# Attention operands through memory, maxima three units ahead, scaled sums early: one change to a tuned attention and gated feed-forward kernel

## The reference, cut to what matters

```
x : 4 x 512 x 512, float32
x = layernorm(x + attention(x))    # 32 query heads of 16, 8 key/value heads: 4 query heads share one
x = layernorm(x + ffn(x))          # 1792 inner rows in blocks of 32; a rank-16 product picks one row per block

attention: q, k, v = x @ wq, x @ wk, x @ wv
           out = softmax(q k^T / 4) v ;  out @ wo
ffn:       inter = x @ c1^T @ c2^T ;  idx = argmax in each block of 32
           h = relu(w1[idx] . x)   ;  out = sum_k h[k] * w2[idx[k]]
```

## Time and profile before

| | us |
|---|---|
| median of three runs | 1025.3 |
| the profiled execution | 1030.88 |
| its span | 1029.1 |
| TensorE's granted clock, mean | 0.895 of 2.4 GHz |

### The profile page before, as it was taken

How to read it: one execution, slowest core, us unless ns; L and a number is a source line. 1 busy time by engine, 2 the same in 40 slices (tenths; PEclk the granted TensorE clock), 3 DMA queues, 4 the chain that set the end, 5 groups by cost and what they waited for, 6 DMA issues and landing times. The chain is left out here.

```text
span 1029.1 us, 12101 instructions
## 1 busy us (share of the span) xinstructions
PE 894.3 (87%) x4344; PEld 528.1 (51%) x4344; DVE 573.5 (56%) x782; ACT 428.3 (42%) x789; POOL 296.7 (29%) x370
## 2 busy tenths in 40 slices
PE   7989888997689889898886546899999999999995
PEld 5755333332233233232324335677777777777774
DVE  6466758876477767776711555643274346426313
ACT  4314655775476656665760101133322222222221
POOL 1002436222333212654630322233421122222221
PEclk9989976988798878878986668999999999999998
DMA  4420522333523333434315245222112003001101
GB/s 143 105 70 3 125 52 59 74 68 70 140 54 67 68 72 58 115 77 97 83 32 153 97 146 172 80 64 82 41 48 75 1 1 103 1 1 42 42 0 41
DMA packets 49243, 72.61 MB, mean 71 GB/s; under 512 B 13888, under 2 KB 18496, under 8 KB 48672
## 3 DMA queue, kind: packets, MB, share of 16 engines
q1 hardware_dynamic: 41552, 65.57, 24.1%
q0 software_dynamic: 7632, 6.28, 2.7%
HBM read 35.31 MB, written 17.56 MB: 51 GB/s over the span
## 5 line engine op out<-in xcount | busy, mean ns | idle before, releaser
L476 DVE TENSOR_REDUCE neg_max<-ps_max 128x2 f32<-128x1024 f32 x256 | 305.9, 1220 | 106.5 <-PE ps_max L589 105.9
L444 ACT ACTIVATE probs<-ps_st 128x512 f32<-128x512 f32 x512 | 270.5, 600 | 147.5 <-PE ps_st L602 145.6
L602 PE MATMUL ps_st<-q,k 50*128 50x512 f32 x512 | 172.8, 539 | 40.6 <-DMA q<-maxima 36.9
L602 PEld LDWEIGHTS ps_st<-q,k 50*128 50x128 f32 x512 | 80.1, 214 | 210.8 <-ACT probs L444 145.1
L616 PE MATMUL ps_pv<-probs,v 128*32 128x512 f32 x1024 | 164.0, 718 | 2.4 <-ACT probs L444 2.4
L291 POOL DMA_DIRECT2D maxima<-max_rows x128 | 77.8, 615 | 265.6 <-DVE max_rows L498 264.9
L846 POOL TENSOR_TENSOR g_l<-picked,g_h 128x512 fp32r<-128x512 f32 x56 | 73.0, 1304 | 269.2 <-ACT g_h L898 269.2
L589 PE MATMUL ps_max<-k,q 48*128 48x512 f32 x512 | 121.2, 488 | 26.1 <-DVE neg_max L476 21.7
L884 ACT ACTIVATE mask_t<-ps_t 128x512 bf16<-128x512 bf16 x56 | 33.4, 597 | 172.7 <-PE ps_t L1113 172.7
L947 DVE TENSOR_REDUCE top<-ps_prep 128x14 f32<-128x448 f32 x62 | 38.6, 623 | 99.7 <-PE ps_prep L1088 99.6
L589 PEld LDWEIGHTS ps_max<-k,q 48*128 48x128 f32 x512 | 62.3, 219 | 58.5 <-DVE neg_max L476 40.2
(11 more groups left out here) (139 smaller groups left out, 1163.2 us busy)
## 6 DMA issues: line engine op xcount, KB each, us to landing
q<-parts SPq DMA_DIRECT2D x192, 64.0 KB, 2.4
sums<-stage SPq DMA_DIRECT2D x32, 256.0 KB, 2.5
k<-parts SPq DMA_DIRECT2D x192, 32.0 KB, 2.0
x_raw<-xT SPq DMA_DIRECT2D x16, 256.0 KB, 4.7
yf<-x SPq DMA_DIRECT2D x4, 1024.0 KB, 5.6
after_attention<-yf SPq DMA_DIRECT2D x4, 1024.0 KB, 10.1
yf<-after_attention SPq DMA_DIRECT2D x4, 1024.0 KB, 5.4
w_raw<-w POOLq DMA_DIRECT2D x16, 224.0 KB, 3.1
```

The costliest lines, as they stand in the source:

```text
L444: nc.scalar.activation(probs[kt % 2][:, r], ps_st[i % 3][:], ACT.Exp, scale=float(HD) ** -0.5).then_inc(exp_done, 1)
L476: nc.vector.tensor_reduce(neg_max[:, at:at + 2], ps_max[pair % 2][:], AX.X, ALU.max, negate=True).then_inc(max_red, 1)
L602: nc.tensor.matmul(ps_st[i % 3][:], k_[n % QR][64 * a:64 * a + ROWS, kt * P:(kt + 1) * P], q[n % QR][64 * a:64 * a + ROWS, j, :], start=Tr ...
```

## The change

1. Operands: after the projections of a batch, SP stores `parts` (high and low of keys and queries, 10 KB rows) to a DRAM buffer `operands`, two DMAs per batch (`store_parts`). A unit is loaded from there by eight DMAs instead of twelve: four on SP (partitions 0 to 47) and four on Pool (partitions 64 to 111). `parts` has two buffers instead of four, so tasks of batch 2 and 3 wait for the stores of batch 0 and 1.
2. `AHEAD = 3`: first passes run three units ahead, with five operand tiles (`QR = 5`). The projections carry 24 pairs instead of 16. The maxima of units 0 and 1 are turned within the projections, and those of unit n + 2 in unit n.
3. The maxima go to DRAM by one DMA instead of four.
4. Denominators are loaded in unit 8b + 9, inverted in 8b + 11, stored and reloaded in 8b + 12 and 8b + 13, for b = 0, 1, 2; Pool scales in unit 8b + 14 and makes both parts in 8b + 15. Only batch 3 is left for the second block, where Pool makes its low part.
5. The w1 splits run one per unit in units 5 to 20.
6. The second block's order changes: denominators are loaded first, both output projections of batch 0 and 1 come first on PE, and Pool's order is root(0), scale, low parts, root(1).

```diff
-    QR = 4
+    QR = 5
+    AHEAD = 3
-    RING = 3 * TILES
-    LOADS = 12
+    RING = (AHEAD + 1) * TILES
+    LOADS = 4
...
+            def store_parts(b):
+                sp.wait_ge(low_out, (REP + 1) * (b + 1))
+                dst = operands[b * PARTS:(b + 1) * PARTS].rearrange("(g h d o t) -> h g d (o t)", g=NKV, h=2, d=HD, t=S)
+                for h in range(2):
+                    sp.dma_start(dst[h], parts[b % 2][:, :, h].bitcast(F32)).then_inc(part_out[b % 2], DMA)
...
             def load_unit(n):
                 if g == 0:
-                    sp.wait_ge(low_out, (REP + 1) * (b + 1))
-                src = parts[b][HD * g:HD * (g + 1)].bitcast(F32)
-                for a in range(2):
-                    for c in range(3):
-                        rows = slice(64 * a + HD * c, 64 * a + HD * (c + 1))
-                        sp.dma_start(k_[j][rows].bitcast(F32), src[:, 0, (0, 0, 1)[c]]).then_inc(unit_in[j], DMA)
-                        sp.dma_start(q[j][rows].bitcast(F32), src[:, 1 + a::2, (0, 1, 0)[c]]).then_inc(unit_in[j], DMA)
+                    sp.wait_ge(part_out[b % 2], 2 * DMA * (b // 2 + 1))
+                at = b * PARTS + g * PARTS // NKV
+                rows = operands[at:at + PARTS // NKV].rearrange("(r o t) -> r o t", r=2 * HD, t=S)
+                for a in (0,):
+                    k_at, q_at = k_[j][64 * a:64 * a + STACK].bitcast(F32), q[j][64 * a:64 * a + STACK].bitcast(F32)
+                    sp.dma_start(k_at[0:2 * HD], rows[0:HD, 0].rearrange("d (c t) -> c d t", c=1).broadcast_to(
+                        [2, HD, S])).then_inc(unit_in[j], DMA)
+                    sp.dma_start(q_at[0:2 * HD], rows[:, 1 + a::2]).then_inc(unit_in[j], DMA)
+                    sp.dma_start(k_at[2 * HD:STACK], rows[HD:2 * HD, 0]).then_inc(unit_in[j], DMA)
+                    sp.dma_start(q_at[2 * HD:STACK], rows[0:HD, 1 + a::2]).then_inc(unit_in[j], DMA)
...
             for k in range(KT):
                 load_x(1, k)
+            store_parts(0)
+            for k in range(KT):
+                load_x(2, k)
             load_unit(0)
             for k in range(KT):
-                load_x(2, k)
+                load_x(3, k)
+            store_parts(1)
             load_unit(1)
             load_unit(2)
-            for k in range(KT):
-                load_x(3, k)
+            store_parts(2)
+            load_unit(3)
+            store_parts(3)
             for n in range(NU):
-                if n + 3 < NU:
-                    load_unit(n + 3)
+                if n + AHEAD + 1 < NU:
+                    load_unit(n + AHEAD + 1)
                 if n:
                     store_unit(n - 1)
-                if n in DEN_AT:
-                    load_den(DEN_AT[n])
-                if n - 1 in DEN_AT:
-                    store_reciprocals(DEN_AT[n - 1])
-                if n == 11:
-                    load_att()
+                b, at = divmod(n - NKV, NKV)
+                if b >= 0 and at == 1:
+                    load_den(b)
+                if b >= 0 and at == 4:
+                    store_reciprocals(b)
+                if b >= 0 and at == 5:
+                    load_att(b)
...
             def send_shift(n):
-                for o in range(4):
-                    pool.dma_start(dst[o], max_rows[32 * o:32 * (o + 1)]).then_inc(max_out, DMA)
-                pool.wait_ge(max_out, 4 * DMA * (n + 1))
+                pool.dma_start(to.rearrange("(c o x) -> o c x", c=32, o=4), max_rows[:]).then_inc(max_out, DMA)
+                pool.wait_ge(max_out, DMA * (n + 1))
...
+            for n in range(AHEAD + 1):
+                load_unit(n)
             send_shift(0)
+            send_shift(1)
             for n in range(NU):
-                if n + 1 < NU:
-                    send_shift(n + 1)
+                if n + AHEAD + 1 < NU:
+                    load_unit(n + AHEAD + 1)
+                if n + 2 < NU:
+                    send_shift(n + 2)
...
-                if n == 12:
-                    scale()
-                if n == 14:
-                    low_att()
-                for i in range(KT * NC):
-                    if 22 + i // 2 == n:
-                        split_w1(i)
+                if 5 <= n < 5 + KT * NC:
+                    split_w1(n - 5)
+                b, at = divmod(n - NKV, NKV)
+                if b >= 0 and at == 6:
+                    scale(b)
+                if b >= 0 and at == 7:
+                    split_att(b)
...
-            for t in range(TT):
-                project_out(0, t)
-            project_out(1, 0)
-            project_out(1, 1)
+            for b in range(2):
+                for t in range(TT):
+                    project_out(b, t)
+            project_out(2, 0)
             front(0)
             front(1)
-            project_out(1, 2)
+            project_out(2, 1)
             front(2)
             front(3)
-            project_out(1, 3)
+            project_out(2, 2)
             front(U)
...
```

More of the change, by code:

```diff
@@ L52 @@
 NU = NB * NKV
+WQ = D + 2 * KV
+PARTS = 2 * P * (REP + 1) * S
 def _scratch(nc, name, n):
@@ L114, in _attend @@
         with ExitStack() as early:
-            x3 = [early.enter_context(nc.sbuf_tensor(f"x_{part}3", [P, KT, S], F32R)) for part in "hl"]
+            first_f = early.enter_context(nc.sbuf_tensor("first_f", [P, P], F32))
         stage = [sb(f"stage{j}", [P, S]) for j in range(2)]
+        with ExitStack() as late:
+            att, inv = [late.enter_context(nc.sbuf_tensor(name, [P, REP, S], F32)) for name in ("att", "inv")]
         wo_raw, c2_raw = sb("wo_raw", [P, REP, D]), sb("c2_raw", [80, INTER])
         c1_raw = sb("c1_raw", [P, KT, 80])
-        w1_raw = [sb(f"w1_raw{j}", [P, CH]) for j in range(2)]
         ps_max = [ps(f"ps_max{j}", [P, 2, S]) for j in range(2)]
@@ L339, in split_w1 @@
                 if i == 0:
-                    pool.wait_ge(att_split, REP)
-                    for j in range(QR):
-                        pool.wait_ge(unit_in[j], LOADS * DMA * (NU - NKV) // QR)
                     load_w1(0)
@@ L402, in take_task @@
                     return
-                nc.scalar.activation(parts[b][:, o, 0], bank(i)[:], ACT.Copy).then_inc(high_out, 1)
+                if b >= 2 and o == 0:
+                    act.wait_ge(part_out[b % 2], 2 * DMA * (b // 2))
+                nc.scalar.activation(parts[b % 2][:, o, 0], bank(i)[:], ACT.Copy).then_inc(high_out, 1)
             def take_sums(n):
@@ L462, in low_task @@
                 dve.wait_ge(high_out, m + 1)
-                nc.vector.tensor_tensor(parts[b][:, o, 1], bank(i)[:], parts[b][:, o, 0].bitcast(F32),
+                if b >= 2 and o == 0:
+                    dve.wait_ge(part_out[b % 2], 2 * DMA * (b // 2))
+                nc.vector.tensor_tensor(parts[b % 2][:, o, 1], bank(i)[:], parts[b % 2][:, o, 0].bitcast(F32),
                                         ALU.subtract).then_inc(low_out, 1)
@@ L634, in _ @@
                     step = n * TT + kt
-                    ahead = 4 * step + 2 * TILES + 1
+                    ahead = 4 * step + AHEAD * TILES + 1
                     scores_t(n, kt, 0)
@@ L728, in w2_tile @@
         def w2_tile(own, late, m):
-            return own[:, m] if m < W2_OWN else late[:, m - W2_OWN]
+            return own[:, W2_OWN - 1 - m] if m < W2_OWN else late[:, m - W2_OWN]
         def number(b, s):
@@ L1222, in build @@
         u = sb("u", [80, S], F32R)
-        sb("to_w1", [P, S])
         w1_h, w1_l = sb("w1_h", [P, KT, INTER], F32R), sb("w1_l", [P, KT, INTER], F32R)
         keep = (w1_h, w1_l, c1_h, c1_l, c2_s, ident, ident16, first, xt_h, xt_l, u, wo_h, wo_l)
-        _attend(nc, xT, w_qkv, wo, c1, c2, w1, (sums, maxima, rden), overlays, keep)
-        _feed_forward(nc, x, x1, out, w2, w2_late, sums, rden, keep)
+        with ExitStack() as under:
+            att_parts2 = [under.enter_context(nc.sbuf_tensor(f"att_{part}2", [P, REP, S], F32R)) for part in "hl"]
+        _attend(nc, xT, w_qkv, wo, c1, c2, w1, (sums, operands, maxima, rden), overlays, keep, att_parts2)
+        _feed_forward(nc, x, x1, out, w2, w2_late, sums, rden, keep, att_parts2)
 def kernel(L0_attn_x, L0_attn_wq, L0_attn_wk, L0_attn_wv, L0_attn_wo, L0_ffn_c1_w, L0_ffn_c2_w, L0_ffn_w1,
```

293 lines of the change are left out of this document (140 added, 153 removed).

## The result

The changed kernel's median is 982.2 us (four runs, 965.2 to 983.0) against 1024.5 us of the kernel before on the same chip: a ratio of 0.959 by the medians. It is faster, as forecast, but the forecast was 922 us. The profiled execution took 965.2 us for a span of 963.5; the forecast for a profiled execution was 928, so 37 us are missing there.

A forecast was written before the change was run, and what follows sets the result against it. Attention was taken as bound by PE's waits for relays and the slow clock that follows, the second block's start by serial relays. Attention -83, projections +6, second block -26 gave 928 us profiled, 922 us median, range 886 to 945 (0.62).

The forecast's parts named there:

- The relay's waits: Attention: PE's 20 waits for reloaded maxima, 36.9 us, go because the relay gets a whole unit more.
- Second block: Start of the second block: one relay of three remains, 106.5 us becomes 80.5, a gain of 26 us.
- Waits, 9 us: Attention: PE waits for late operand loads, 1, 1 and 4 us from Pool's lag plus 3 for unit 4's operands.
- The store's term: Attention: 3 us of waiting for unit 4's operands, whose SP half stands behind the last store of projections.
- Clock, 8 us plus 10 at the end: Attention: slow clock costs 2 us after each of four waits, plus 10 us for seven possibly slow last steps.
- Projections, +6: Projections: input-tile wait of 5.9 us goes, eight more pairs add 4.6, delays behind stores add 7; 15 us per batch store.
- the +12: Projections: alternative cost of about 12 us if batch stores run on eight engines and take 19.8 us.
- (a): Attention: Pool's full queue sets the pace, +35 to +50 us, 957 to 972; chance 0.29 together with (c).
- (b): Attention: Pool's issues of operand loads cost far more, about 1100 us at 3 us each; slower, chance 0.06.
- (c): Attention: slow clock has its own cause and comes without waits, +42 us, 964; chance 0.29 together with (a).
- (d): Attention and second block: late operand loads replace relay waits one for one, nothing gained, about 1030 us; chance 0.03.
- (e): Attention: splitting loads between SP and Pool gives away about 10 us; inside the forecast, no separate chance.

The follow-up runs named there:

- scaling spread: Changed kernel with Pool's scaling and splitting of batches 0 and 1 spread over six units: 958.9 us, ratio 0.936 to the kernel before.
- sums head by head: Changed kernel with sums and broadcast reciprocals loaded by head, 8 + 8 DMAs instead of 4 + 1: 971.8 us, ratio 0.948 to the kernel before.
- small preparations: Changed kernel with Pool's wo, c1, c2 preparation in pieces over units 1 to 8, w1 splits in units 9 to 24: 978.0 us, ratio 0.948.
- second profile: Changed kernel run once more without edit, beside two combined kernels: median 982.5 us, ratio 0.956, profiled execution 985.9 us.

## Why the prediction was half right

**Direction and mechanism: right.** The relay's waits are gone, and the run with two units ahead shows that this is the third unit's doing. A unit that waits for nothing takes 10.6 to 11.2 us, as forecast (10.7), in 20 of 32.

**Second block: right.** 78.6 us against 80.5.

**Waits, 9 us: the step that failed.** 33 were measured. The step counted Pool's lag and the last store of the projections. The store's term came out (unit 0 waits 2.8 us, 3 stood), in part by luck: the same wait is 6.2, 6.6 and 7.5 us in three kernels with the same start (scaling spread, sums head by head, small preparations). Of Pool's, unit 16 lost 6.8 us where 4 stood, and unit 15 1.7; but the late loads of units 5 and 6 that were expected for Pool's long preparations didn't come, and unit 2 lost 4.8 us instead, behind the 1.4 MB of wo, c1 and c2. Two things were left out, both to be seen before. One is bytes ahead of loads with a deadline: these 1.4 MB, and the 2 MB of sums and reciprocals, which now move inside attention for three batches: 4.8 and 2.7 us, or 8.3 and 7.2 with all loads in one queue. The prediction counted SP's issues ("cannot be late") and not its bytes. The other is DVE's small operations beside Pool's long ones, 4.6 us in unit 5. The kernel before has them too (its cast took 2.26 us at 162.1, its subtraction 3.01 at 165.5), and they make the fourth of its waits for DVE, 1.9 us; the prediction explained three of the four and let all 17.4 us go.

**Clock, 8 us plus 10 at the end: mis-sized, and of two kinds.** After the waits it was 28 us in the first profile: about 80 us of slow clock for seven places with waits, 12 each, where the mean of the kernel before, 6, was taken for four. A long wait has more of it than a short one: 17 us around unit 16's wait of 6.8. The 20.5 us in unit 0, which begin ahead of its wait, are in this sum; with 61 us the other six have 10 each. The 10 us for the end were 0 in the first profile and 11 in the second. The step's sign and place were right; that it comes in some executions only was not foreseen and could not be from one profile. Of the signs that the prediction named for its being wrong, the first stood at the edge (attention over 400 us: 399.5 in the first profile, 417.7 in the second), and the second came: the clock fell with no wait ahead of it, in unit 0, and in the second profile in unit 30.

**Projections, +6: +14 measured.** The store takes 20.7 us instead of 15, and task 12 waits 7.0 us and unit 1's maxima 4.7 for it. By the +12 that the prediction gave beside the Trainium skill's rule, this term would have been within 2 us.

**Rivals.** (a) as a pace falls, though its time of 957 to 972 held the profiled execution: the number was right for another reason, and of the waits for operands only 8.4 us are Pool's late issues. (b) falls: Pool's issues of the new loads take 0.5 to 0.85 us, a median of 0.54. (c), whose 964 came within 2 us of the profiled execution, holds for the last two units in some executions and perhaps for unit 0, not for the rest. (d) falls: the relay's waits were not replaced one for one. (e) holds in its mechanism; its price, about 6 us of attention by the run with all loads on SP where 10 were named, is less than what two profiles of one kernel differ by.

## What to carry to other kernels

When a change moves a bulk transfer into a stretch with small loads on a deadline, count the bytes ahead of each load, not only the issues: the wait shrinks with the size of the block. Cut blocks (a transfer, a run of operations on Pool) to what fits into one unit's slack, and expect a part of the gain only until the last cause of a late load is gone. And price a wait with the slow clock behind it: here some 4 us for each wait of 2 to 7 in the first profile.

## What the runs showed of the hardware

- DVE's cast of 128x16 from SBUF to SBUF took 3.0 us beside Pool's tensor operations and ended with them, through two that follow each other (L351 and L352), where its median is 0.17. The Trainium skill (SBUF — State Buffer, Who interferes with whom) says that in such pairs whichever was issued first holds the shared ports for its whole instruction; the trace agrees, and shows that a waiting DVE operation can miss the gap between two of Pool's. DVE's reductions from PSUM kept their 1.2 us.
- SP's issue of a load of 64 KB took 7.5 us behind a store of 1.3 MB per DMA (58.67 above), and 7.2 and 8.4 after the next ones, instead of 0.6. Pool's stores of maxima beside them (81.2 and 112.4) landed some 6 us after their issue, where they take 1.8 when little else moves. With the same bytes as sixteen DMAs of 160 KB no such issue took over 1.9 us, but the sixteen themselves took 13.5. An issue on SP is not a fixed price.
- TensorE's granted clock fell to 0.50 in units 30 and 31 with no wait ahead in one execution and stayed at 1.00 in another, same kernel, same instructions. Of the eleven profiles of kernels with three units ahead, seven had it fall in the last two units before the last exponential began. What decides it stays open.
